# Half of the out projection between the halves of the gate projection, decayed B in front of the outputs, in a Mamba-style recurrent layer on Trainium2

## The chip, the cores and the metric

The kernel runs on one core of one Trainium2 chip. A core has a matrix engine (TensorE, PE in the profile), three engines that work on 128 partitions (VectorE or DVE, ScalarE or ACT, GpSimd or POOL) and a queue for transfers (SyncE or SP). Each runs its own instructions in program order, and they wait for one another on semaphores. The metric is the time of one execution on the device in microseconds; the smaller the better.

## What is computed

`u` has 4 sequences of 1024 tokens with 128 features. Each token is normalised and projected to a gate z and an input x of 2048 channels each (32 heads of 64), to B and C (64 each), and to angles, step sizes and mixing weights per head. Then, cut to what matters here:

```python
Bm, Cm = rope(_rms(Braw) + B_bias), rope(_rms(Craw) + C_bias)   # rotated by cumulative angles, per head
def step(carry, inp):
    h, prevBx = carry
    x_t, B_t, C_t, a_t, g_t, b_t = inp
    Bx = jnp.einsum('bhp,bhn->bhpn', x_t, B_t)
    h = a_t[..., None, None] * h + g_t[..., None, None] * Bx + b_t[..., None, None] * prevBx
    return (h, Bx), jnp.einsum('bhpn,bhn->bhp', h, C_t)
y = y + xh * D
y = y * silu(z)
y = _rms(y, norm_w)
s = y @ out_proj_w.T
out = u + s * silu(fp8_linear(xn))
```

## The kernel before

`prepare` does what is done once (normalisation, small projections, running sums of decays). `units` is the main loop and takes nearly all of the time. It cuts the 4096 tokens into NS = 8 tiles `t` of 512 tokens, each of four chunks of 128, and the 32 heads into NQ = 8 groups `q` of four heads, that is two pairs p = 0 and 1. There are 64 iterations (t, q). Two tiles make a sequence: an even tile begins one (its first chunk has no state to add), an odd tile ends one.

The recurrence is done by chunks. Per iteration the engines do this, each in the order written out by hand in its block:

- **VectorE**: `rotation` (L1299) makes the parts of rotated B and C: `part` from `bcs` and `trig`, both in SBUF, eight per iteration, for the next group. `angles` (L1274) reduces the angles of the group after that. `state` (L1373) carries the state over chunks, in six to eight small instructions. `x_scaled` (L1283) makes `xc` from x. `scores` (L1317) multiplies scores by decays to `M`, four per iteration (0, 1 are made one iteration ahead). L1412 makes `yT`, output times silu(z), one for each pair. `b_decayed` (L1309) makes `bw`, B times decay, two for the next group. `norm_start`, `norm_seeded` and `norm_refined` are small instructions for the norm of the tile before, in the iterations q = 0.
- **PE**: `angles` (L1107), the chunk states (L1193), `exponents` (L1127, one per head), `scores` (L1138, sixteen matmuls per pair), `x_by_token` (L1112, two halves), `project` (L1153, the out projection of the group before), z (L1221, two halves, one PSUM bank each, `R[0]` and `R[1]`, which x uses before them), the outputs y (L1229, L1235, L1245), and `b_by_token` (L1118), the transposes of rotated B. `square_sums` (L1164) adds the squares over partitions, once per tile.
- **ACT**: `decays` (L1458, to `E`), `x_copy` (L1463), silu of z (L1505), `sines` (L1447 to L1453), `rounding` (L1443), `squares` (L1468, of `yT`).
- **POOL**: `sums` (L1527) adds two parts to `rot`, four per iteration; `c_decayed` (L1536) makes `ce` from `rot` and `eb`, two; L1571 adds the squares to `sqa`, two (L1564 for q = 0, where it is one).
- **SP** issues the transfers: `spread` (trig, eight per iteration), `load_eb`, `load_rows` and others.

Around the change the order on VectorE is, for an iteration (t, q): rotation 0 of the next group, `angles`, `state`, rotation 1, xc 0, M 2, M 3, xc 1, rotations 2 to 7, yT 0, yT 1, bw 0, bw 1, M 0, M 1 of the next group. In the prediction, A is the first of these rotations and B the second. VectorE's semaphore waits for M are on `e_ready` (ACT's decay) and `s_ready` (PE's scores); for bw on `bt_ready`; for yT on `y_ready`, `sz_ready`, `out_ready`, `sq_ready`. z half p waits for `xk_ready`, that is for xc p, which reads the same bank.

## Time and profile before

| | us |
|---|---|
| median of 3 runs | 1199.95 (1198.5 to 1201.43) |
| the profiled execution | 1202.91 |
| its span, from first to last instruction | 1201.0 |
| PE busy | 1130.3 (94%) |
| DVE busy | 1131.8 (94%) |
| ACT busy | 818.6 (68%) |
| POOL busy | 755.2 (63%) |
| mean granted TensorE clock | 0.969 of full |

The main loop begins at about 145 us and ends at about 1195. A row of the timeline gives the start of an instruction in us from the span's start, how long it lasted (several of one kind that follow one another are one row, with their number behind the x), its engine, its line, what it writes and reads, and in brackets the idle time of the engine before it with what ended that. An instruction that had to wait for the shared SBUF access after it was issued shows this as a longer duration, and not as idle time. Engines issue an instruction some 0.04 to 0.08 us before the one ahead has ended, so two rows of an engine may overlap by that much.

### The profile page before, as it was taken

Reading aid. Unit: us, or ns where it says so; the run is one execution under the profiler, and the core shown is the slowest. Engines: PE = TensorE matmul, PEld = TensorE weight load, DVE = VectorE, ACT = ScalarE, POOL = GpSimd, SP = SyncE. Lnnn points to the kernel's source line nnn. Section 1 sums busy time; section 2 is a strip of 40 time slices with the busy share of each in tenths; the row PEclk is TensorE's granted clock in tenths of the full one; section 3 lists DMA queues with packets and bytes.
Section 4 is the critical chain, followed back from the end, with each engine's and each line's share of the span. In section 5 each row is a group of like instructions: output and inputs, shape, how many; then the busy total and the mean of one; then the engine's idle time right before and its main releaser. Section 6 shows DMA issues by size and latency. Waiting matters only on the chain.

```text
span 1201.0 us, 30402 instructions
## 1 busy us (share of the span) xinstructions
PE 1130.3 (94%) x11442; PEld 822.0 (68%) x11442; DVE 1131.8 (94%) x1796; ACT 818.6 (68%) x1270; POOL 755.2 (63%) x560
## 2 busy tenths in 40 slices
PE   3899599999999999999999999999999999999996
PEld 3673467777777777677777777777777777777675
DVE  7878599999999999999999999999999999999994
ACT  4678366767676676777666777667766766776663
POOL 5000256776776667666777677776766687767774
PEclk9956699999999999999999999999999999999999
DMA  8645645444545464545554464546544545444450
GB/s 184 213 137 123 146 108 115 117 113 110 139 100 115 106 152 106 125 97 124 125 124 106 101 148 101 123 111 145 115 108 103 136 115 125 107 93 99 111 120 15
DMA packets 91888, 142.94 MB, mean 119 GB/s; under 512 B 19326, under 2 KB 38591, under 8 KB 91327
## 3 DMA queue, kind: packets, MB, share of 16 engines
q1 hardware_dynamic: 91743, 141.00, 50.3%
q8 instruction: 91, 1.49, 0.5%
q14 instruction: 54, 0.44, 0.1%
HBM read 58.68 MB, written 13.37 MB: 60 GB/s over the span
## 4 chain that ended last, share of the span: by engine, by line
PE 56%; DVE 19%; issue 8%; DMA 2%; ACT 1%; SPq 1%; POOL 0%; DVEq 0%; POOLq 0%; ACTq 0%
PE y L1235 10%; PE r L1221 8%; PE s L1138 6%; PE y L1229 5%; PE r L1118 5%; PE o L1153 5%; PE y L1245 5%; PE r L1112 4%; DVE M L1317 4%; DVE hs L1373 4%; DVE xc L1283 3%; DVE bw L1309 3%; PE r L1193 2%; PE r L1107 2%; PE d L1127 2%
## 5 line engine op out<-in xcount | busy, mean ns | idle before, releaser
L1527 POOL TENSOR_TENSOR rot<-part 128x512 f32<-128x512 f32 x256 | 383.9, 1500 | 310.8 <-DVE part L1299 310.8
L1299 DVE SCALAR_TENSOR_TENSOR part<-k_bcs,k_prmT,k_trig 128x512 f32<-128x512 f32 x512 | 527.1, 1077 | 9.2 <-SPq L1047 6.3
L1458 ACT ACTIVATE E<-d 128x512 f32<-128x512 f32 x256 | 152.9, 597 | 184.4 <-PE d L1127 184.1
L1536 POOL TENSOR_TENSOR ce<-rot,eb 128x512 f32<-128x512 f32 x128 | 185.5, 1468 | 2.3 <-POOLq L1566 2.1
L1317 DVE TENSOR_TENSOR M<-s,E 128x512 f32<-128x512 f32 x256 | 163.6, 677 | 1.9 <-PE s L1138 1.4
L1571 POOL TENSOR_TENSOR sqa<-sqa,sq 128x512 f32<-128x512 f32 x112 | 142.7, 1274 | 31.7 <-ACT sq L1468 23.1
L1138 PE MATMUL s<-rot 64*128 64x128 f32 x2048 | 149.2, 285 | 0.0
L1138 PEld LDWEIGHTS s<-rot 64*128 64x128 f32 x2048 | 124.7, 188 | 35.2 <-issue 34.8
L1112 PE MATMUL r<-k_w_zx,k_xns 128*128 128x256 f32 x512 | 136.8, 391 | 11.8 <-issue 6.3
L1463 ACT COPY xk<-r 128x512 f32<-128x512 f32 x128 | 75.2, 587 | 104.7 <-PE r L1112 104.6
L1235 PE MATMUL y<-M,xk 128*64 128x128 f32 x2048 | 140.1, 279 | 0.0
L1153 PEld LDWEIGHTS o<-k_w_o,yT 128*128 128x128 f32 x1024 | 132.8, 192 | 8.5 <-DVE yT L1412 1.7
L1221 PE MATMUL r<-k_xns,k_w_zx 128*128 128x512 f32 x256 | 133.3, 614 | 4.0 <-DVE xc L1283 1.8
L1153 PE MATMUL o<-k_w_o,yT 128*128 128x128 f32 x1024 | 133.4, 275 | 1.4 <-DVE yT L1412 1.4
L1235 PEld LDWEIGHTS y<-M,xk 128*64 128x64 f32 x2048 | 109.2, 136 | 21.5 <-issue 21.5
L1112 PEld LDWEIGHTS r<-k_w_zx,k_xns 128*128 128x128 f32 x512 | 90.4, 192 | 30.3 <-DVE ang L1274 8.5
L1127 PE MATMUL d<-k_cum,k_pick 123*128 123x512 bf16 x256 | 99.4, 388 | 0.0
L1505 ACT ACTIVATE sz<-r 128x512 f32<-128x512 f32 x128 | 75.7, 597 | 33.0 <-PE r L1221 32.4
L1283 DVE TENSOR_TENSOR xc<-r,k_cc 128x512 f32<-128x512 f32 x128 | 87.2, 681 | 4.6 <-ACT xk L1463 4.6
L1193 PEld LDWEIGHTS r<-xk,bw 128*64 128x64 f32 x1792 | 57.5, 137 | 48.8 <-DVE bw L1309 47.3
L1229 PEld LDWEIGHTS y<-k_ident,xc 128*128 128x128 f32 x512 | 58.8, 140 | 44.7 <-issue 44.7
L1412 DVE TENSOR_TENSOR yT<-y,sz 128x512 f32<-128x512 f32 x128 | 81.7, 677 | 6.3 <-PE y L1245 6.3
(247 smaller groups left out, 1673.2 us busy)
## 6 DMA issues: line engine op xcount, KB each, us to landing
k_trig<-k_tri SPq DMA_DIRECT2D x512, 128.0 KB, 2.4
eb<-ecum_rows SPq DMA_DIRECT2D x128, 256.0 KB, 4.7
k_bcs<-bc_t SPq DMA_DIRECT2D x16, 256.0 KB, 3.9
k_bcs<-bc_t SPq DMA_DIRECT2D x32, 128.0 KB, 3.8
k_bcs<-in_L_attn_u SPq DMA_DIRECT2D x4, 512.0 KB, 6.4
xn_t<-a_xnT SPq DMA_DIRECT2D x1, 2048.0 KB, 12.7
tc_t<-a_tcT SPq DMA_DIRECT2D x1, 2048.0 KB, 17.2
bc_t<-a_tmp SPq DMA_DIRECT2D x1, 2048.0 KB, 7.5
```

The lines of the kernel that those rows point to most:

```text
L1112: last = nc.tensor.matmul(R[i][:, 256 * c:256 * c + 256], xns[:, (t + q // NQ) % 2, (2 * i + c) * P:(2 * i + c + 1) * P], K["w_zx"][:, DI ...
L1127: nc.tensor.matmul(Dp[:], K["pick"][:, head * P:head * P + P], K["cum"][0:D_ROWS, q % 2, h, :], start=True, stop=True).then_inc(d_ready, 1)
L1138: last = nc.tensor.matmul(Sp[j][:, k], rot[rows, q % 2, p, 0, k], rot[rows, q % 2, p, 1, k], start=True, stop=True)
L1153: last = nc.tensor.matmul(Op[:, k], yT[:, p, k], K["w_o"][:, (2 * q + p) * P:(2 * q + p + 1) * P], start=False, stop=q == NQ - 1 and c == ...
L1221: nc.tensor.matmul(R[p][:], w, xns[:, t % 2, :], start=True, stop=True).then_inc(z_ready, 1)
L1235: nc.tensor.matmul(Yp[p][m:m + 64, k], xk[:, par, c, 128 * p + m:128 * p + m + 64], M[:, 2 * p + j, k], start=False, stop=c == 0 and begin ...
L1299: nc.vector.scalar_tensor_tensor(out=part[:, 2 * p + f, :], in0=bcs[:, (t + q // NQ) % 2, 2 * w + f, :], scalar=col, in1=trig[:, p, 1 - f, ...
L1317: nc.vector.tensor_tensor(M[:, h, :], Sp[h % 2][:], E[:, h % 2, :], ALU.mult).then_inc(m_ready, 1)
L1458: nc.scalar.activation(E[:, h % 2, :], Dp[:], ACT.Exp).then_inc(e_ready, 1)
L1527: nc.gpsimd.tensor_tensor(rot[:, q % 2, p, w, :], part[:, 2 * p, :], part[:, 2 * p + 1, :], ALU.add).then_inc(rot_ready, 1)
L1536: nc.gpsimd.tensor_tensor(ce[:, p, :], rot[:, q % 2, p, 1, :], eb[:, p, :], ALU.mult).then_inc(ce_ready, 1)
L1571: nc.gpsimd.tensor_tensor(sqa[:], sqa[:], sq[:, p, :], ALU.add).then_inc(sqa_ready, 1)
```

## The change

No instruction is added or removed; five orders change.

- PE: `project(t, q - 1, (2, 3))`, half of the out projection (all of it for q = 1), stands between the two halves of z instead of ahead of both. `square_sums(t - 1)`, in the iterations q = 0, stands behind the first half of `project` instead of ahead of `x_by_token`.
- VectorE: `b_decayed` stands ahead of yT, and M 0, yT 0, M 1, yT 1 alternate. In q = 0 `norm_start` stands behind `x_scaled(…, 1)`, and the last `norm_refined` behind yT 0.
- ACT: `decays(q + 1, 1)` stands ahead of both squares. `rounding` is done for q + 3 between the two squares, where it was done for q + 2 at the start of the next iteration.
- POOL: `c_decayed` of the next group stands directly behind its sums and ahead of the additions of squares, where it stood behind them.

```diff
@@ tensor
-                    if q == 0 and t > 0:
-                        square_sums(t - 1)
                     if live(t, q + 1):
...
                         x_by_token(t, q + 1, 0)
                     if t + q > 0 and q != 1:
                         project(t, q - 1, (0, 1))
+                    if q == 0 and t > 0:
+                        square_sums(t - 1)
                     pe.wait_ge(hch, at(T8, t, 8 * q + 8))
                     if live(t, q + 1):
                         x_by_token(t, q + 1, 1)
-                    if t + q > 0:
-                        project(t, q - 1, (2, 3) if q != 1 else range(CS))
                     for p in range(2):
-
+                        if p == 1 and t + q > 0:
+                            project(t, q - 1, (2, 3) if q != 1 else range(CS))
                         if live(t, q + 1):
                             pe.wait_ge(xk_ready, at(T2, t, 2 * q + 2 + p + 1))
@@ vector
+                    if live(t, q + 1):
+                        x_scaled(t, q + 1, tn, 1)
                     if q == 0 and t > 0:
                         norm_start(t - 1)
-                    if live(t, q + 1):
-                        x_scaled(t, q + 1, tn, 1)
...
+                    if live(t, q + 1):
+                        b_decayed(t, q + 1, tn)
                     for p in range(2):
+                        if live(t, q + 1):
+                            scores(t, q + 1, p)
                         dve.wait_ge(sz_ready, at(T2, t, 2 * q + p + 1))
...
                         nc.vector.tensor_tensor(yT[:, p, :], Yp[p][:], sz[:, p, :], ALU.mult).then_inc(yt_ready, 1)
-                    if q == 0 and t > 0:
-                        norm_refined(t - 1, 2)
-                    if live(t, q + 1):
-                        b_decayed(t, q + 1, tn)
-                    if live(t, q + 1):
-                        scores(t, q + 1, 0)
-                        scores(t, q + 1, 1)
+                        if p == 0 and q == 0 and t > 0:
+                            norm_refined(t - 1, 2)
@@ scalar
+            rounding(0, 2)
             for t in range(NS):
                 for q in range(NQ):
-                    if live(t, q + 2):
-                        rounding(t, q + 2)
...
                     if live(t, q + 1):
                         decays(t, q + 1, 0)
+                        decays(t, q + 1, 1)
                     squares(t, q, 0)
-                    if live(t, q + 1):
-                        decays(t, q + 1, 1)
+                    if live(t, q + 3):
+                        rounding(t, q + 3)
                     squares(t, q, 1)
@@ gpsimd
+            c_decayed(0, 0)
             for t in range(NS):
                 for q in range(NQ):
-                    c_decayed(t, q)
                     if live(t, q + 1):
                         for k in range(4):
                             sums(t, q + 1, k)
...
+                        c_decayed(*((t, q + 1) if q < NQ - 1 else (t + 1, 0)))
                     if q == 0:
```

## Rows read from the trace of the kernel before

**Rows 1.** Windows: length, busy (count) of PE, PEld, DVE, ACT, POOL; clock, DMA share, GB/s.
```profile
614.06:630.36 16.30, 16.16 (x170) 11.62 (x170) 15.75 (x26) 11.15 (x18) 11.44 (x8) 1.00 0.51 129
745.06:761.23 16.17, 16.04 (x171) 11.64 (x170) 16.06 (x28) 11.30 (x18) 11.44 (x8) 1.00 0.56 133
```

**Rows 2.** Timeline of DVE in the iteration in an odd tile (start, duration, instruction).
```profile
613.98 6.09 DVE L1299 SCALAR_TENSOR_TENSOR part<-k_bcs,k_prmT,k_trig 128x512 f32<-128x512 f32 x6
620.00 1.28 DVE L1412 TENSOR_TENSOR yT<-y,sz 128x512 f32<-128x512 f32 x2
...
624.08 0.97 DVE L1299 SCALAR_TENSOR_TENSOR part<-k_bcs,k_prmT,k_trig 128x512 f32<-128x512 f32 x1 [0.41 <-DMA k_trig<-k_tri]
...
627.03 0.93 DVE L1299 SCALAR_TENSOR_TENSOR part<-k_bcs,k_prmT,k_trig 128x512 f32<-128x512 f32 x1
```

**Rows 3.** The same timeline, of POOL.
```profile
615.46 1.73 POOL L1527 TENSOR_TENSOR rot<-part 128x512 f32<-128x512 f32 x1 [2.44 <-DVE part L1299]
...
620.15 1.28 POOL L1527 TENSOR_TENSOR rot<-part 128x512 f32<-128x512 f32 x1 [0.63 <-DVE part L1299]
621.81 2.69 POOL L1571 TENSOR_TENSOR sqa<-sqa,sq 128x512 f32<-128x512 f32 x2 [0.38 <-ACT sq L1468]
624.47 2.95 POOL L1536 TENSOR_TENSOR ce<-rot,eb 128x512 f32<-128x512 f32 x2
```

**Rows 4.** The fourth of the six rotations of rows 2, alone.
```profile
615.96 1.77 DVE L1299 SCALAR_TENSOR_TENSOR part<-k_bcs,k_prmT,k_trig 128x512 f32<-128x512 f32 x1
```

**Rows 5.** Timeline of PE and ACT in the same iteration.
```profile
620.51 1.16 PE L1138 MATMUL s<-rot 64*128 64x128 f32 x16
622.03 0.60 ACT L1458 ACTIVATE E<-d 128x512 f32<-128x512 f32 x1 [0.30 <-PE d L1127]
622.53 0.62 ACT L1468 ACTIVATE sq<-yT 128x512 f32<-128x512 f32 x1
625.71 1.13 PE L1112 MATMUL r<-k_w_zx,k_xns 128*128 128x256 f32 x4
...
629.32 2.22 PE L1221 MATMUL r<-k_xns,k_w_zx 128*128 128x512 f32 x4
```

**Rows 6.** Timeline around 492 us, DVE and POOL.
```profile
492.30 1.84 DVE L1299 SCALAR_TENSOR_TENSOR part<-k_bcs,k_prmT,k_trig 128x512 f32<-128x512 f32 x1 [0.55 <-DMA k_trig<-k_tri]
492.33 2.94 POOL L1536 TENSOR_TENSOR ce<-rot,eb 128x512 f32<-128x512 f32 x2
```

**Rows 7.** Timeline of the start of the loop.
```profile
141.39 1.26 POOL L1527 TENSOR_TENSOR rot<-part 128x512 f32<-128x512 f32 x1 [0.63 <-DVE part L1299]
...
142.78 2.49 POOL L1536 TENSOR_TENSOR ce<-rot,eb 128x512 f32<-128x512 f32 x2
...
145.03 1.65 PE L1138 MATMUL s<-rot 64*128 64x128 f32 x16
...
146.76 0.69 DVE L1317 TENSOR_TENSOR M<-s,E 128x512 f32<-128x512 f32 x1 [1.36 <-PE s L1138]
```

**Rows 8.** Timeline of the iteration in an even tile.
```profile
751.30 1.16 PE L1138 MATMUL s<-rot 64*128 64x128 f32 x16
...
754.58 1.27 DVE L1299 SCALAR_TENSOR_TENSOR part<-k_bcs,k_prmT,k_trig 128x512 f32<-128x512 f32 x1
...
758.09 0.74 DVE L1299 SCALAR_TENSOR_TENSOR part<-k_bcs,k_prmT,k_trig 128x512 f32<-128x512 f32 x1
```

**Rows 9.** Timeline of a tile start, iterations q = 0 and 1.
```profile
267.84 0.68 DVE L1283 TENSOR_TENSOR xc<-r,k_cc 128x512 f32<-128x512 f32 x1
...
279.94 0.95 PE L1164 MATMUL y<-k_ones,sqa 128*128 128x1 f32 x8
...
284.39 0.68 DVE L1283 TENSOR_TENSOR xc<-r,k_cc 128x512 f32<-128x512 f32 x1
...
300.94 0.68 DVE L1283 TENSOR_TENSOR xc<-r,k_cc 128x512 f32<-128x512 f32 x1
301.51 1.88 PE L1221 MATMUL r<-k_xns,k_w_zx 128*128 128x512 f32 x4
```

## The prediction

> **What bounds the kernel now.** I read the totals first [rows 1]: within one iteration of the main loop TensorE is busy 16.16 of 16.30 us and VectorE 15.75. Two engines are full at once, so what matters is the loop of waits that joins them, and I read one iteration engine by engine. The profile calls the engines PE (TensorE), DVE (VectorE), ACT (ScalarE), POOL (GpSimd) and SP (SyncE). I count time inside an iteration from the end of its `x_scaled(…, 1)` (below: xc1): 614.06 in an odd tile, 745.06 in an even one. The two stretches of rows 1 run from there to the next xc1's end, so an iteration takes 16.30 and 16.17 us.
>
> The reader is to see three things in these rows.
>
> First, the eight `rotation` instructions don't cost one price. Undisturbed, one takes 0.74 [rows 8], and the six after xc1 would take 4.0 at that price; they took 6.09 [rows 2]. The fourth after xc1 took 1.77: it was issued at 615.96, while POOL's sum ran from 615.46 to 617.19 [rows 3, 4], and it ended 0.55 after that sum. A rotation reads two SBUF tiles, a POOL addition too, and in these rows one stands still until the other is through. POOL pays as well: 1.73 for that sum, 1.28 for the one at 620.15 with no rotation beside it. VectorE's other operations (yT, bw, M, xc, which read one PSUM tile) keep their 0.68 and follow one another every 0.60, also beside POOL: the two yT at 620.00 took 1.28 while POOL ran its sum of 620.15 [rows 2, 3]. So the order in which VectorE and POOL come to the shared access is a cost of its own.
>
> Second, the rotation that opens an iteration, A, is the one in question. It was issued at 624.08, while POOL added the squares (621.81 to 624.50), and ended at 625.05, again 0.55 behind POOL [rows 2, 3]. Although POOL's ce was next in its queue at 624.47, A went first, as it had been waiting: ce took 2.95 for two, not about 2.5.
>
> Third, what places the end of that addition: scores on PE end at 621.67, the last decay on ACT 622.03 to 622.63, the second square 622.53 to 623.15, then the addition, then A, and from A's end VectorE runs without a gap to xc1, which releases the second half of z [rows 2, 3, 5]. This is the loop: z, y, scores, decay, square, addition, A, xc1, 16.3 us.
>
> **What the change does to it, part by part.** PE: half of `project` goes between the halves of z. No instruction is added. The second half of z waits for xc1 as before, so PE only fills a wait of about 0.3 us there (the z group took 2.22 for four [rows 5], and 1.88 where nothing held it [rows 9]), and it is worth nothing while xc1 comes last. I take 0, bounds -0.3 and 0. The first silu on ACT comes earlier, and nothing waits for it.
>
> ACT: `rounding(q+3)` goes between the squares and `decays(q+1, 1)` ahead of both. Rounding needs PE's `angles(q+3)`, which needs only bw 0, now early; squares follow yT. The second square slips behind yT 1, and the decay that follows it by about 0.6 us; PE uses that decay only before its `x_by_token`, which waits longer for A. 0. SP: no DMA is added. `load_eb` waits for ce, which is now ready earlier in the iteration; SP comes to it after the eight spreading DMAs as before, and there is over half an iteration until the next ce. The k_trig transfer can hold A (0.41 us of idle at 624.08 [rows 2]) but A now comes at 10.1 against 10.02 there, so this falls away or lies under what holds A below: 0.
>
> VectorE: the order after the rotations was yT 0, yT 1, bw 0, bw 1, M 0, M 1, A. It becomes bw 0, bw 1, M 0, yT 0, M 1, yT 1, A. The same six operations, but M 0 now comes third and meets a wait that the trace of before does not show: it needs the scores. VectorE would be ready at 5.94 + 1.20 = 7.14 [rows 2]. The sixteen score matmuls end at 621.67 - 614.06 = 7.61 in an odd tile and 752.46 - 745.06 = 7.40 in an even one [rows 5, 8]. From the end of such a group to M it was 146.76 - 146.68 = 0.08 at the start of the loop, the one place where M waited for scores [rows 7]. So M 0 starts at 7.69 (odd), 7.48 (even), a wait of 0.55 and 0.34. Then yT 0, M 1, yT 1 and A follow at 0.60 each: **A is issued at 10.09 and 9.88**. In before it was ready to go at about 9.5 (9.52 even [rows 8]). The queue behind M 0 is the whole of VectorE. Bounds for this wait alone: 0 (if the scores are seen before 7.14) and 0.6.
>
> POOL: ce moves from behind the squares' additions to directly behind the sums. The last sum ends at 620.15 + 1.28 - 614.06 = 7.37 [rows 3]; the even tile has the same, as its rotations end at the same place (A issued at 9.52, six operations of 0.60 before it: 5.92 [rows 8], against 5.94). How ce follows a sum directly is shown at the start: sum ends 142.65, ce starts 142.78, two take 2.49 [rows 7]. So **ce ends at 9.99**, and the first addition of squares can be issued at about 9.95 (POOL issues 0.03 to 0.04 ahead of an end: 624.47 against 624.50 [rows 3]). It is ready by then: yT 0 ends at 7.69 + 0.60 + 0.68 = 8.97, its square takes 0.62 [rows 5] and the hand-overs about 0.12, so 9.7.
>
> So the new orders bring A (10.09 and 9.88) and the first addition of squares (9.95) to the shared access at the same moment. In the odd tile the addition is first by 0.14. In the even tile A is issued 0.07 before it. Which wins there is told by one event in the trace: at 492.30 a late rotation was issued 0.03 ahead of POOL's ce at 492.33, and lost. It took 1.84, to 494.14, which is 0.55 after ce's first half [rows 6]. A blocked rotation ends 0.55 after its release, an undisturbed one 0.74 after its issue, so it seems to ask only some 0.19 after its issue: 10.07 in the even tile, too late against 9.99. I take it that A loses in both.
>
> The Trainium skill (SBUF — State Buffer, "Who interferes with whom") calls this an exclusive lock between VectorE operations with two SBUF inputs and GpSimd, where "Issue order, not op shape, decides who blocks." The blocked rotations agree with the lock; the pair at 492.30 does not agree with a literal issue order. By that sentence A would pass in even tiles, which is the first rival below.
>
> If A loses, the addition runs 9.95 to 11.22 and A ends at 11.77, in both kinds of tile. Before: 10.99 odd, 10.79 even. From A's end to B, the second rotation, 1.98 odd and 2.24 even; B now undisturbed at 0.74 (odd: was 0.93, held by ce, so 0.19 comes back); from B's end to xc1's end 2.40 [rows 1, 2, 8].
> - odd: 11.77 + 1.98 + 0.74 + 2.40 = 16.89, against 16.30: **+0.59**
> - even: 11.77 + 2.24 + 0.74 + 2.40 = 17.15, against 16.17: **+0.98**
>
> PE is not the limit: it now waits about 0.9 for A's follower before `x_by_token`.
>
> Tile starts: `square_sums` (0.95 of PE [rows 9]) now stands after half of `project`. With A late, PE goes from 12.4 (behind VectorE's `angles`, 0.68, that follows A) through x, out, x, out (625.71 to 629.32, 3.6 [rows 5]), the sums (0.95) and half of z (0.9) to z 1 at 17.8. Before, this iteration took 16.55 from xc1 to xc1 (268.52 to 285.07 [rows 9]): +1.2. In the next one (301.62 - 285.07 = 16.55 too) z already ended 1.77 behind xc1 (303.39) instead of 1.2, so 17.1 from z to z. There all of `project` now stands between the z halves, and z 0 waits for xc 0, which waits for ACT's copy behind `normalised`: an estimate of 17.6, +0.5. POOL has only one addition in that iteration, which waits for the second square, so A passes. The iteration after makes good 0.2. Together +1.5 per start; bounds 0.5 and 2.5.
>
> **Sum.** Even tiles have 4 x 6 such iterations (q = 2 to 7), odd tiles 3 x 6, and the last 5: 24 x 0.98 = 23.5 and 23 x 0.59 = 13.6; seven starts x 1.5 = 10.5; the accident at 492.30 (that iteration was 1.2 longer) goes: -1.2. Total +46.4. The profiled execution took 1202.9, 3.0 over the median of 1199.95; so 1249.3 profiled and **1246 us** for the median.
>
> **Rivals.**
> - *A passes in even tiles.* A ends at 9.99 + 0.55 = 10.54, xc1 at 10.54 + 2.24 + 0.74 + 2.40 = 15.92: -0.25 an iteration, about what PE still allows: it was idle only 0.14 of 16.30 by its records [rows 1], beside the wait in the z group. 24 x -0.25 in place of 23.5 gives 1217. As PE then comes after xc1 by up to 0.1, the next A is issued at 9.98 and loses; if they alternate, 1231. For it: the margin is 0.07 to 0.19 us. Against it: 492.30. Chance 0.14.
> - *A passes everywhere.* Odd: A 10.09 to 10.83, B is held by the second addition; about -0.15; even -0.25; starts +1.3 each for PE's reason: 1200, no change. Needs POOL 0.14 to 0.3 later than the startup row says. Chance 0.05.
> - *Faster: M 0 does not wait.* If the scores are ready for M 0 at 7.14, A is issued at 9.54, is already waiting when ce ends at 9.99, and passes ahead of the addition as at 624.50. It ends at 10.54, and both kinds of iteration fall to what PE allows, about 16.0: 23 x -0.3 + 24 x -0.17 = -11, and starts at +0.8: +5.6. 1194 to 1195. It decides at an A issued before about 9.8, that is scores 0.1 (even) to 0.3 (odd) us earlier than their rows. Against it: those rows are the same in all iterations but tile starts. With other ways to be faster that I don't see, chance 0.15.
> - *Slower still*: tile starts at their upper bound, or the second addition takes B too: 1254 to 1262. Chance 0.06.
>
> **How the numbers follow.** Forecast 0.60, rivals as given. About 0.2% (2.4 us) is what a measurement of this kernel tells from no change. Slower: 0.60 + 0.14 + 0.06 = 0.80; same 0.05; faster 0.15. The likeliest case alone spans 1236 to 1256 (starts, and 0.1 us on each iteration). The range for 8 in 10 reaches down through the even-tile rival: 1210 to 1256.
>
> **What would show it.** In the profile after: M 0 with an idle time of 0.3 to 0.6 released by PE's scores; A lasting 1.6 to 1.9 instead of 0.97 to 1.27, beside the first addition of squares; ce 2.5 for two, directly behind the last sum; B at 0.74; iterations of 16.9 (odd) and 17.15 (even) with PE idle 0.8 to 0.9 before `x_by_token`. It is wrong if A shows under 1.3 in most iterations, or if M 0 has no idle time.

## The result, and the profile after

| | before | after |
|---|---|---|
| median (runs) | 1200.69 (1196.88 to 1205.29, 6) | 1228.52 (1225.74 to 1234.78, 6) |
| ratio, with its 95% interval | | 1.0242 (1.0214 to 1.027) |
| span of the profiled execution | 1201.0 | 1232.6 |

The change makes the kernel 2.4% slower. That is inside the range of 1210 to 1256, but 17.5 us below the forecast of 1246 and outside the 1236 to 1256 that the prediction gave to its likeliest case. The first lines of the page of after, then four groups of its section 5:

```profile
span 1232.6 us, 30401 instructions
PE 1124.6 (91%) x11442; PEld 824.1 (67%) x11442; DVE 1132.8 (92%) x1796; ACT 819.5 (66%) x1270; POOL 749.7 (61%) x560
...
L1298 DVE SCALAR_TENSOR_TENSOR part<-k_bcs,k_prmT,k_trig 128x512 f32<-128x512 f32 x512 | 518.1, 1058 | 6.5 <-SPq L1047 6.3
...
L1316 DVE TENSOR_TENSOR M<-s,E 128x512 f32<-128x512 f32 x256 | 169.5, 682 | 23.4 <-issue 21.4
L1570 POOL TENSOR_TENSOR sqa<-sqa,sq 128x512 f32<-128x512 f32 x112 | 162.1, 1448 | 22.3 <-ACT sq L1466 14.3
L1534 POOL TENSOR_TENSOR ce<-rot,eb 128x512 f32<-128x512 f32 x128 | 160.7, 1277 | 8.5
```

Busy times hardly differ from those of before; what has grown is idle time. The line to look at is M: 23.4 us of idle time in front of it, nearly all put down to issue. Before, it was 1.9:

```profile
L1317 DVE TENSOR_TENSOR M<-s,E 128x512 f32<-128x512 f32 x256 | 163.6, 677 | 1.9 <-PE s L1138 1.4
```

In after no instruction is named as the releaser, but the timelines below put M's start 0.09 behind the end of the scores: it is the wait that the prediction spoke of. ce takes 1.28 each: POOL's ce is no longer beside a rotation.

The whole spans are not good to compare. The loop begins (end of the first xc1) at 137.7 us in before and at 141.6 in after; over the profiles of this case it begins anywhere from 131.4 to 141.6, and the TensorE clock granted in the first 131 us goes with it (0.77 in before, 0.76 in after, 0.82 in e6, which begins at 131.4). So from here on I sum the loop alone, from the end of the first xc1 to that of the last: 1032.46 before, 1059.50 after, **+27.0**, which agrees with the +27.8 between the medians. Iteration by iteration (63 of them, from one xc1 end to the next; groups of four heads by q):

| part of the loop | before, each | after, each | predicted, sum | measured, sum |
|---|---|---|---|---|
| odd tiles, q = 3 to 7 (19) | 16.30 | 16.91 (mean) | +11.2 | +11.5 |
| even tiles, q = 3 to 7 (20) | 16.17 and one of 17.39 | 16.12 | +18.4 | -2.1 |
| q = 0, 1 and 2 (24) | 16.59 (mean) | 17.33 (mean) | +16.8 | +17.6 |
| all | | | +46.4 | +27.0 |

(The predicted sums are those of the prediction, distributed: 19 x 0.59; 20 x 0.98 less the accident's 1.2; the starts' 10.5 with 4 x 0.98 + 4 x 0.59 for q = 2.) The odd tiles came out as worked out, the even tiles did not lose at all, and the third line is near only as a sum, as the section on the prediction shows.

Windows of one iteration in an odd and one in an even tile of after, columns as in [rows 1]:

```profile
628.23:645.13 16.90, 15.93 (x172) 11.67 (x171) 16.32 (x27) 11.20 (x18) 11.24 (x8) 1.00 0.51 126
763.40:779.51 16.11, 15.82 (x172) 11.69 (x171) 15.71 (x27) 11.18 (x17) 11.52 (x8) 1.00 0.55 128
```

The odd one, timeline of VectorE and POOL, with PE's scores and x (xc1 ends at 628.23), answering to [rows 2, 3, 5]:

```profile
634.32 1.27 POOL L1525 TENSOR_TENSOR rot<-part 128x512 f32<-128x512 f32 x1 [0.63 <-DVE part L1298]
...
634.69 1.16 PE L1138 MATMUL s<-rot 64*128 64x128 f32 x16
...
635.72 2.51 POOL L1534 TENSOR_TENSOR ce<-rot,eb 128x512 f32<-128x512 f32 x2
...
635.94 0.69 DVE L1316 TENSOR_TENSOR M<-s,E 128x512 f32<-128x512 f32 x1 [0.44 <-issue]
...
638.20 2.94 POOL L1570 TENSOR_TENSOR sqa<-sqa,sq 128x512 f32<-128x512 f32 x2
638.34 1.67 DVE L1298 SCALAR_TENSOR_TENSOR part<-k_bcs,k_prmT,k_trig 128x512 f32<-128x512 f32 x1
...
640.66 1.13 PE L1112 MATMUL r<-k_w_zx,k_xns 128*128 128x256 f32 x4 [0.64 <-DVE ang L1273]
...
641.99 0.74 DVE L1298 SCALAR_TENSOR_TENSOR part<-k_bcs,k_prmT,k_trig 128x512 f32<-128x512 f32 x1
```

The even one (xc1 ends at 763.40), answering to [rows 8]:

```profile
769.64 1.16 PE L1138 MATMUL s<-rot 64*128 64x128 f32 x16
...
770.88 2.51 POOL L1534 TENSOR_TENSOR ce<-rot,eb 128x512 f32<-128x512 f32 x2
770.89 0.69 DVE L1316 TENSOR_TENSOR M<-s,E 128x512 f32<-128x512 f32 x1 [0.29 <-issue]
...
773.29 0.74 DVE L1298 SCALAR_TENSOR_TENSOR part<-k_bcs,k_prmT,k_trig 128x512 f32<-128x512 f32 x1
...
773.34 3.23 POOL L1570 TENSOR_TENSOR sqa<-sqa,sq 128x512 f32<-128x512 f32 x2
...
776.27 0.85 DVE L1298 SCALAR_TENSOR_TENSOR part<-k_bcs,k_prmT,k_trig 128x512 f32<-128x512 f32 x1
```

Read the two side by side. In the odd tile the addition of squares is issued at 638.20 and A at 638.34. A is second: it takes 1.67 and ends, at 640.01, 0.54 after the first addition (638.20 + 1.27). PE waits 0.64 behind VectorE's `angles`, and the iteration is 16.9. In the even tile A is issued at 773.29, 0.05 ahead of the addition's 773.34. A takes 0.74, and it is the addition that pays (3.23 for two). In the even tile B also pays a little (0.85), held by the second addition.

### The profile page after: what moved, and what is told of

Read it like the earlier page. It is cut to its first block, busy times and chain, and to the rows that moved or that the text cites. A ratio compares the mean times of both kernels' runs of the same rounds, so it can differ in the third digit from the quotient of the medians.

```text
span 1232.6 us, 30401 instructions
## 1 busy us (share of the span) xinstructions
PE 1124.6 (91%) x11442; PEld 824.1 (67%) x11442; DVE 1132.8 (92%) x1796; ACT 819.5 (66%) x1270; POOL 749.7 (61%) x560
## 4 chain that ended last, share of the span: by engine, by line
PE 54%; DVE 16%; issue 14%; ACT 2%; DVEq 1%; DMA 0%; POOL 0%; SPq 0%; POOLq 0%; ACTq 0%
PE y L1234 10%; PE r L1220 10%; PE o L1153 7%; PE y L1228 5%; PE r L1118 5%; PE y L1244 5%; PE r L1112 5%; DVE yT L1415 4%; PE s L1138 4%; DVE ang L1273 3%; DVE hs L1372 2%; DVE xc L1282 2%; DVE M L1316 2%; PE d L1127 1%; DVE part L1298 1%
## 5 line engine op out<-in xcount | busy, mean ns | idle before, releaser
L1298 DVE SCALAR_TENSOR_TENSOR part<-k_bcs,k_prmT,k_trig 128x512 f32<-128x512 f32 x512 | 518.1, 1058 | 6.5 <-SPq L1047 6.3
L1316 DVE TENSOR_TENSOR M<-s,E 128x512 f32<-128x512 f32 x256 | 169.5, 682 | 23.4 <-issue 21.4
L1570 POOL TENSOR_TENSOR sqa<-sqa,sq 128x512 f32<-128x512 f32 x112 | 162.1, 1448 | 22.3 <-ACT sq L1466 14.3
L1534 POOL TENSOR_TENSOR ce<-rot,eb 128x512 f32<-128x512 f32 x128 | 160.7, 1277 | 8.5
L1220 PE MATMUL r<-k_xns,k_w_zx 128*128 128x512 f32 x256 | 138.6, 623 | 8.5 <-DVE xc L1282 7.4
L1127 PE MATMUL d<-k_cum,k_pick 123*128 123x512 bf16 x256 | 99.5, 389 | 15.8 <-ACT E L1456 13.2
L1466 ACT ACTIVATE sq<-yT 128x512 f32<-128x512 f32 x128 | 80.7, 631 | 39.2 <-DVE yT L1415 38.9
L1415 DVE TENSOR_TENSOR yT<-y,sz 128x512 f32<-128x512 f32 x128 | 86.9, 679 | 6.3 <-PE y L1244 6.3
L1308 DVE TENSOR_TENSOR bw<-r,k_dec 128x512 f32<-128x512 f32 x128 | 82.0, 679 | 10.2 <-PE r L1118 10.1
```

The costliest lines, as they stand in the source:

```text
L1220: nc.tensor.matmul(R[p][:], w, xns[:, t % 2, :], start=True, stop=True).then_inc(z_ready, 1)
L1298: nc.vector.scalar_tensor_tensor(out=part[:, 2 * p + f, :], in0=bcs[:, (t + q // NQ) % 2, 2 * w + f, :], scalar=col, in1=trig[:, p, 1 - f, ...
L1316: nc.vector.tensor_tensor(M[:, h, :], Sp[h % 2][:], E[:, h % 2, :], ALU.mult).then_inc(m_ready, 1)
L1415: nc.vector.tensor_tensor(yT[:, p, :], Yp[p][:], sz[:, p, :], ALU.mult).then_inc(yt_ready, 1)
L1534: nc.gpsimd.tensor_tensor(ce[:, p, :], rot[:, q % 2, p, 1, :], eb[:, p, :], ALU.mult).then_inc(ce_ready, 1)
L1570: nc.gpsimd.tensor_tensor(sqa[:], sqa[:], sq[:, p, :], ALU.add).then_inc(sqa_ready, 1)
```

## The experiments

Ratios are against the kernel before, in the same job, with 95% intervals; loop sums are from the profile of each kernel. "Lost" and "passed" are said of A at the shared access.

**e1: M behind yT.** The change with one order undone: VectorE does yT 0, M 0, yT 1, M 1, so that nothing waits for scores ahead of yT.

```diff
                     for p in range(2):
-                        if live(t, q + 1):
-                            scores(t, q + 1, p)
...
                         nc.vector.tensor_tensor(yT[:, p, :], Yp[p][:], sz[:, p, :], ALU.mult).then_inc(yt_ready, 1)
...
+                        if live(t, q + 1):
+                            scores(t, q + 1, p)
```

> The changed kernel, with yT 0, M 0, yT 1, M 1 on VectorE in place of M 0, yT 0, M 1, yT 1. Theory (the loss in odd tiles is the wait of M 0 for the scores, which makes A miss the shared access): M 0 is due at 7.74 and finds its scores; A is issued at 9.54, waits for ce to end at 9.99 and passes ahead of the addition, ends at 10.54. B is then held by the second addition to 13.5, so iterations of odd and even tiles both go to 15.9 to 16.1 (now 16.91 and 16.12). About 17 to 20 us less than the changed kernel, about 1210. Rival (half of project between the halves of z costs the time, by making z and so y later): odd iterations stay at 16.9, 1228.

Measured: 1205.4 (1203.48 to 1212.33, 5 runs), ratio 1.0071 (1.0041 to 1.0101). The loop sum is 1036.80: 22.7 of the 27.0 are gone with this one order, where 17 to 20 were expected. By the ratios of the whole times it is 1.7% of the 2.4%, about 20 us. Odd and even iterations from q = 3 on are 16.03 to 16.20, but for two of 16.91 (odd) and one of 17.17 (even). Such a single one and its neighbour, timeline of VectorE and POOL:

```profile
623.81 2.94 POOL L1570 TENSOR_TENSOR sqa<-sqa,sq 128x512 f32<-128x512 f32 x2
623.83 1.79 DVE L1298 SCALAR_TENSOR_TENSOR part<-k_bcs,k_prmT,k_trig 128x512 f32<-128x512 f32 x1 [0.33 <-DMA k_trig<-k_tri]
...
638.53 0.68 DVE L1316 TENSOR_TENSOR M<-s,E 128x512 f32<-128x512 f32 x1
...
640.33 0.98 DVE L1298 SCALAR_TENSOR_TENSOR part<-k_bcs,k_prmT,k_trig 128x512 f32<-128x512 f32 x1
...
640.72 3.14 POOL L1570 TENSOR_TENSOR sqa<-sqa,sq 128x512 f32<-128x512 f32 x2
```

The M at 638.53 has no idle time in front. A at 640.33 comes 0.39 ahead of the addition; it waits for ce to end and passes. At 623.83 a transfer of trig kept A for 0.33, it came 0.02 behind the addition, and took 1.79. So a delay of A by 0.33 makes an iteration 0.86 longer: this is the mechanism of the forecast, once with the wait and once without.

**e2: the addition waits for both squares.** The change as it is, but POOL's first addition of squares comes later, so that A is first in every tile.

```diff
-                        pool.wait_ge(sq_ready, at(T2, t, 2 * q + p + 1))
+                        pool.wait_ge(sq_ready, at(T2, t, 2 * q + 2))
```

> The changed kernel, with the first addition of squares on POOL waiting for both squares instead of one. Nothing is faster by itself, and M 0 still waits for the scores. Theory (A loses the shared access to an addition issued 0.14 us ahead of it): the addition now comes at 10.9, A (10.11) passes and ends at 10.85 in odd tiles too; the second addition then holds B to about 14.0, so odd iterations 16.4 (now 16.91), even ones 16.1 to 16.2 (now 16.12): 8 to 10 us less, about 1219. Rival (the wait of M 0 alone makes the loss, whoever passes first): odd iterations stay at 16.9 or grow.

Measured: 1223.23 (1222.83 to 1226.76, 4 runs), ratio 1.0214 (1.0188 to 1.024); loop sum 1053.34, 6.2 less than the change, where 8 to 10 were expected. Odd iterations 16.56 (16.91 in the change; 16.4 expected), even 16.34 (16.12). Timeline of an odd one:

```profile
618.25 0.74 DVE L1298 SCALAR_TENSOR_TENSOR part<-k_bcs,k_prmT,k_trig 128x512 f32<-128x512 f32 x1
...
619.07 2.68 POOL L1570 TENSOR_TENSOR sqa<-sqa,sq 128x512 f32<-128x512 f32 x2 [0.85 <-ACT sq L1466]
...
620.97 1.33 DVE L1298 SCALAR_TENSOR_TENSOR part<-k_bcs,k_prmT,k_trig 128x512 f32<-128x512 f32 x1
```

A passes (0.74) in the iterations from q = 3 on, which is the cause tested. But the two additions now run 619.07 to 621.75 and B, at 620.97, stands 0.59 for the second. The cost of the shared access has moved to the next instruction of VectorE that needs it. The loop is still 20.9 longer than before although A never loses: 6.5 of it from q = 3 on, 14.4 in q = 0 to 2.

**e3: POOL's order alone.** The kernel before, with ce directly behind the sums.

```diff
                 sums(0, 0, k)
+            c_decayed(0, 0)
             for t in range(NS):
                 for q in range(NQ):
-                    c_decayed(t, q)
...
+                        c_decayed(*((t, q + 1) if q < NQ - 1 else (t + 1, 0)))
                     if q == 0:
```

> The kernel before, with ce behind the sums and ahead of the additions on POOL, and nothing else. Theory: A is issued at 9.52, waits for ce to 9.99, ends at 10.54 in place of 10.99 and 10.79; the two additions then run to 13.0 and hold B to 13.5. Iterations 15.9 to 16.1 in both kinds of tile, 0.1 to 0.3 less than before: 8 to 15 us less than before, about 1188. Rival (ce early is itself a part of the loss): slower than before, by up to the 17 us that odd tiles lost.

Measured: 1213.34 (1213.15 to 1224.1, 4 runs), ratio 1.0147 (1.01 to 1.0193). From q = 3 on iterations take 16.03 to 16.15 but for three of 16.90 to 17.00, as expected; the total is not. The loop is 14.2 longer than before, and more than all of that is in q = 0, where from the second tile on iterations take 18.45 to 20.0. Timeline of one, POOL and PE:

```profile
274.05 3.12 POOL L1572 TENSOR_TENSOR sqa<-sqa,sq 128x512 f32<-128x512 f32 x2
...
277.31 1.02 PE L1164 MATMUL y<-k_ones,sqa 128*128 128x1 f32 x8 [1.66 <-POOL sqa L1572]
```

The additions end at 277.17 and PE, which needs them for `square_sums` ahead of `x_by_token`, has stood idle for 1.66. This edge was missing from my expectation. It is what the change moves `square_sums` for.

**e9: POOL's order with the sums of squares later.** e3, with `square_sums` behind the first half of `project` and `norm_start` behind xc1, as in the change; VectorE's orders around M, yT and bw, ACT's and z's stay those of before.

```diff
-                    if q == 0 and t > 0:
-                        square_sums(t - 1)
...
                         project(t, q - 1, (0, 1))
+                    if q == 0 and t > 0:
+                        square_sums(t - 1)
```

> The kernel before, with ce ahead of the additions on POOL, square_sums behind the first half of project and norm_start behind x_scaled; VectorE's order of yT, bw and M, ACT's order and project as before. Theory: the iterations q = 3 to 7 stay at 16.05 (with ce alone they were 16.05, before 16.16 and 16.30), and q = 0, which took 18.5 to 20.0 with ce alone as PE waited there for the additions, goes to 16.6 to 16.9. 6 to 10 us less than before, 1190. Rival (q = 0 loses for another reason): it stays above 18.

Measured: 1195.39 (1190.21 to 1202.93, 12 runs), ratio 0.9977 (0.995 to 1.0004); loop sum 1024.20, 8.3 less than before. q = 0 takes 16.6 to 16.7 from the second tile on, and q = 2 to 7 take 16.02 to 16.14 but for one of 17.17. By the one profile this part of the change gains 0.22 an iteration in odd tiles and 0.09 in even ones besides the accident; in the whole time that is at the edge of what can be told, as the interval reaches 1. Executions with the same granted clock agree on the sign: at 0.975, three of e9 took 1190.21 to 1192.68 and seven of before 1196.48 to 1199.36.

**e4, e8, e11: A put off by a small operation.** The change, with a memset on VectorE ahead of A, of 32, 160 and 320 columns, that nothing else uses. This is to find where between "0.05 ahead" and "0.14 behind" A begins to lose.

```diff
+        pad = sb("pad", [P, 160])
...
                             norm_refined(t - 1, 2)
+                    nc.vector.memset(pad[:], 0.0)
```

> The changed kernel, with one memset of a small unused tile (32 columns) on VectorE ahead of A in each iteration, about 0.1 us. Theory (in even tiles A passes only because it is issued 0.07 ahead of the addition): A comes at 10.0, loses, and even iterations jump from 16.12 to 17.1 to 17.2, twenty-odd times; odd ones by 0.1 at most. 20 us more than the changed kernel, about 1250. Rival (even tiles pass for another reason, for instance because they have no carried state to add): both kinds grow by the 0.1 us of the memset, 5 to 6 us in all, about 1234.

> The changed kernel with a memset of 160 columns ahead of A on VectorE, which should take about 0.2 and put A off by about 0.15, where the one of 32 columns put it off by only some 0.04. Theory: A is now issued behind the addition in even tiles too, and loses: even iterations go from 16.13 to 17.1 to 17.3, odd ones from 16.91 by at most 0.15. 20 us more than the changed kernel. Rival: both kinds grow by 0.15.

> The changed kernel with a memset of 320 columns ahead of A (about 0.33 us by the 0.19 of 160 columns and 0.085 of 32). With 160 columns A still passed in even tiles except in the first tile, where it was 0.1 us behind the addition and those iterations took 17.17 against 16.17. Theory: A is now behind by 0.15 or more everywhere, loses everywhere, and the even iterations q = 3 to 7 of all tiles take 17.2 to 17.4; odd ones stay near 16.9 to 17.1, as they lost already. Rival (the first tile differs for another reason): the even iterations of the later tiles grow by the 0.13 of the memset alone, to 16.3.

Measured: e4 1230.16 (1227.6 to 1239.49, 4 runs), ratio 1.0289 (1.0238 to 1.0341): the memset put A off by only about 0.04, A stayed 0.03 to 0.05 ahead of the addition in most even iterations (0.10 to 0.13 in the others that passed), and those stayed at 16.13 to 16.19; two of the twenty lost (17.17 and 17.25). That is a miss by itself. e8: 1241.72 (2 runs), ratio 1.0351 (1.0298 to 1.0403). e11, 1 run: 1235.21. The loop sums are 1063.15, 1065.67 and 1069.77, that is 3.6, 6.2 and 10.3 over the change. Timeline of two even iterations of e8:

```profile
219.69 0.19 DVE L1419 MEMSET pad<- 128x160 f32 x1
219.70 2.96 POOL L1572 TENSOR_TENSOR sqa<-sqa,sq 128x512 f32<-128x512 f32 x2
219.80 1.72 DVE L1299 SCALAR_TENSOR_TENSOR part<-k_bcs,k_prmT,k_trig 128x512 f32<-128x512 f32 x1
...
747.46 0.19 DVE L1419 MEMSET pad<- 128x160 f32 x1
747.53 3.20 POOL L1572 TENSOR_TENSOR sqa<-sqa,sq 128x512 f32<-128x512 f32 x2
747.57 0.63 DVE L1299 SCALAR_TENSOR_TENSOR part<-k_bcs,k_prmT,k_trig 128x512 f32<-128x512 f32 x1
```

At 219.80 A is 0.10 behind and loses, as in the even iterations of tile 0 (17.17). At 747.57 it is 0.04 behind and passes, as in those of tiles 2, 4 and 6 (16.17). In e11 17 of the 20 even iterations were 16.34, with A 0.18 or more behind; I had expected 17.2 to 17.4 there. Over all iterations of a kernel, by the recorded starts, A needs to be 0.03 ahead in e4, may be 0.10 behind in e8 and 0.27 behind in e11. In e8 the start of the memset tells it better. Of the iterations where it lies within 0.25 of POOL's, A passed in 18 of 18 where the memset began 9 ns or more ahead, and lost in all 28 where it began less than 5 ns ahead (as at 219.69, which the rows round to 0.01) or behind; in e11 the boundary is at a memset some 0.03 behind, with two exceptions. So behind a memset A's own start does not say when the access was claimed.

The memset alone does not hold the access for A. Where A's last transfer of trig was late, A lost although the memset was well ahead. The even iteration of 17.25 in e4, timeline of VectorE and POOL:

```profile
1003.78 0.09 DVE L1419 MEMSET pad<- 128x32 f32 x1
...
1003.90 1.83 DVE L1299 SCALAR_TENSOR_TENSOR part<-k_bcs,k_prmT,k_trig 128x512 f32<-128x512 f32 x1
1003.91 1.27 POOL L1572 TENSOR_TENSOR sqa<-sqa,sq 128x512 f32<-128x512 f32 x1
```

The memset began 0.13 ahead of the addition, but the last packet of trig landed only at 1003.87, and A lost. The two exceptions of e11 are of the same kind: at 736.29 the memset began 0.06 ahead of the addition, as in five iterations that passed, but in these trig had landed 0.28 or more before the memset, and here it landed with the memset's start. By these rows A's claim needs A's own data, and it can be made while the memset still runs; A's duration fits that (0.74 alone, 0.72 behind 32 columns, 0.63 behind 160 and 320). What sets the moment of the claim there is **open**.

**e5: the out projection back.** The change, with all of `project` ahead of both halves of z again.

```diff
+                    if t + q > 0:
+                        project(t, q - 1, (2, 3) if q != 1 else range(CS))
                     for p in range(2):
-                        if p == 1 and t + q > 0:
-                            project(t, q - 1, (2, 3) if q != 1 else range(CS))
```

> The changed kernel, with all of the second part of project ahead of both halves of z again, as before the change. Theory (the project between the halves costs nothing in most iterations, but in q = 1, where all 16 matmuls stand there, it makes z 1 late and with it the next iteration): odd iterations q = 3 to 7 stay at 16.85 to 16.91 and even ones at 16.1; q = 1 goes from 17.69 (odd) to about 17.0 and q = 2 from 17.75 to 16.9 (odd) and 17.79 to 16.2 (even). 8 to 12 us less than the changed kernel. Rival (project between the halves is what costs the odd iterations): they fall to 16.3, and 20 us or more are gained.

Measured: 1225.86 (1220.84 to 1229.21, 4 runs), ratio 1.0215 (1.0175 to 1.0254); loop sum 3.9 less than the change. Odd iterations stay 16.91 and even ones, but for one of 17.18, 16.12: the place of `project` has no part in them. q = 2 gives 5.2 (odd tiles 17.75, now 16.91 to 17.26; even ones 17.8 to 18.1, now 17.2 to 17.6, where A still loses), and the one of 17.18 takes 1.1 of it. A saving of 8 to 12 was expected.

**e6: e1, and for q = 1 the out projection ahead of z.**

```diff
+                    if q == 1:
+                        project(t, q - 1, range(CS))
                     for p in range(2):
-                        if p == 1 and t + q > 0:
-                            project(t, q - 1, (2, 3) if q != 1 else range(CS))
+                        if p == 1 and t + q > 0 and q != 1:
+                            project(t, q - 1, (2, 3))
```

> The variant with yT ahead of M, and besides for q = 1 alone all of project ahead of both halves of z. Theory: q = 1 goes from 16.98 to about 16.6 and q = 2 from 17.2 to 16.1, seven and eight times, all else as it was: 9 to 11 us less than without this, 1195, level with the kernel before or 0.3% faster. Rival (the tile starts lose for the later square_sums): q = 1 and 2 stay, and q = 0 is where the time is.

Measured: 1197.54 (1191.67 to 1203.97, 12 runs), ratio 0.9989 (0.9966 to 1.0012); loop sum 1027.48, 9.3 less than e1 and 5.0 less than before. q = 2 went from 17.2 to 16.1, but for two (16.91, 17.16). q = 1 stayed at 16.98 to 17.01, where 16.6 was expected.

**e10: the last norm instruction behind M 1.** e6, with `norm_refined(t - 1, 2)` behind both M. This asks what holds q = 1.

```diff
-                        if p == 0 and q == 0 and t > 0:
-                            norm_refined(t - 1, 2)
                         if live(t, q + 1):
                             scores(t, q + 1, p)
+                    if q == 0 and t > 0:
+                        norm_refined(t - 1, 2)
```

> The variant with yT ahead of M and project of q = 1 ahead of z, with the last norm_refined (128x4) behind M 1 in place of behind yT 0. Theory (this small instruction reads two SBUF tiles, and ce on POOL holds it for about 1 us at a tile start): it costs under 0.3 there, and the iterations q = 1 go from 16.98 to 16.6 or less, seven times; the others stay. Rival (the 17.0 of q = 1 is due to PE's project and ACT's normalised): they stay at 17.0.

Measured, 1 run: 1204.47; odd tiles' q = 1 fell from 16.98 to 16.13 in three of four. But other iterations grew (17.39 in even tiles' q = 1; 16.91 to 17.2 in q = 2, and one of 18.47), and the loop sum is 1034.01, 6.5 over e6. In the odd tiles the term is shown; without it the queue meets other collisions elsewhere.

**e12 and e13: the second addition of squares in the next iteration.** e9, with POOL's second addition behind the first sum of the next iteration; e13 also has half of `project` between the halves of z, but for q = 1.

```diff
                             sums(t, q + 1, k)
+                            if k == 0 and q > 1:
+                                added(t, q - 1, 1)
...
-                    for p in range(2):
...
+                    for p in range(2 if q == NQ - 1 else 1):
+                        added(t, q, p)
```

> The kernel before with ce ahead of the additions, square_sums and norm_start later, and besides the second addition of squares on POOL behind the first sum of the next iteration (for q = 1 to 6). Theory: in the variant without this, B is held by the second addition, which ends at 13.0; with it gone B ends at 13.3 in place of 13.5 to 13.7, and iterations go from 16.05 to between 15.85 and 16.0, where PE alone sets them. 3 to 8 us less than that variant, 1187 to 1192, ratio 0.990 to 0.995. Rival (PE sets the 16.05 already): no change.

> The one before, with half of project between the halves of z, except for q = 1. Theory: with VectorE no longer late, PE's wait for xc 1 between the z halves (up to 0.3 us) is what the split fills: 0 to 0.15 per iteration less than without it, so 0 to 8 us. Rival (the split is worth nothing, as z 1 still waits for xc 1, or costs): same or slower.

Measured: e12 1199.91 (12 runs), ratio 0.9991 (0.9971 to 1.0011); e13 1200.85 (12 runs), ratio 1.0002 (0.9983 to 1.0021). e12 misses the expectation of 0.990 to 0.995: its loop sum is 1031.51, 7.3 more than e9. e13, expected 0 to 8 below e12, has 1033.47. In odd tiles q = 5 to 7 take 15.77 (16.05 in e9), with the split and without it but for two that grew, so the split of `project`, the first item of the change, is worth nothing here either. In tiles after the first, q = 3 and 4 grow to 16.77 and 17.03. Timeline of POOL around one in tile 1, and the second of VectorE's six rotations there:

```profile
328.73 1.27 POOL L1527 TENSOR_TENSOR rot<-part 128x512 f32<-128x512 f32 x1 [1.67 <-DVE part L1299]
...
329.96 1.27 POOL L1554 TENSOR_TENSOR sqa<-sqa,sq 128x512 f32<-128x512 f32 x1
...
331.19 1.72 POOL L1548 TENSOR_TENSOR res<-so,res 128x512 f32<-128x512 f32 x1
...
331.70 1.76 DVE L1299 SCALAR_TENSOR_TENSOR part<-k_bcs,k_prmT,k_trig 128x512 f32<-128x512 f32 x1
```

There the last operations of the tile before (`so` and `res`) come behind the same sum, and the addition pushes them back. In e9 `res` starts at 328.51, beside xc and M, and VectorE's second rotation takes 0.74; here it starts at 331.19, and that rotation stands until 0.55 behind its end. That is the 1.0 by which these iterations are longer than q = 5 to 7. In tile 0 there are none, and its q = 3 and 4 take 16.03.

## Why the prediction came out as it did

**M 0 waits for the scores: right.** Predicted at 7.69 (odd) and 7.48 (even) from xc1's end; measured 635.94 - 628.23 = 7.71 and 770.89 - 763.40 = 7.49. e1 shows that this wait is what costs: without it 22.7 of the loop's 27.0 us go. The 0.08 from the start of the loop [rows 7] was a good price for a wait that the loop did not show.

**Odd tiles: right, for the reason given.** Predicted: A issued at 10.09, addition at 9.95, A's end at 11.77, iteration 16.89. Measured: 10.11, 9.97, 11.78, 16.90. The rule "0.55 behind the release" held, and B was undisturbed at 0.74.

**Even tiles: wrong. The failed step is the one that read a single event.** The positions were right (A at 9.88, measured 773.29 - 763.40 = 9.89; addition at 9.94). From the rotation at 492.30, issued 0.03 ahead of ce and beaten [rows 6], I inferred that a rotation asks for the access only some 0.19 after its issue, and so gave A the loss at a lead of 0.07. In the twenty even iterations from q = 3 on A led by 0.05 to 0.17 (14 of them by 0.05 to 0.08) and passed. The 0.19 was the difference of two durations (0.74 and 0.55), and no row showed it as a time of asking; the event itself said only that a lead of 0.03 is too little. The eleven traces without a memset have 164 rotations that start within 0.2 us of a POOL operation other than the sums:

| start of the rotation | passed | lost |
|---|---|---|
| behind, or up to 0.04 ahead | 0 | 85 |
| 0.05 or 0.06 ahead | 6 | 1 |
| 0.07 to 0.2 ahead | 72 | 0 |

Nine of the 85 were 0.02 to 0.04 ahead, as at 492.30. The one exception and one that passed at the same lead, timelines of e1 and of e6:

```profile
408.54 1.87 DVE L1298 SCALAR_TENSOR_TENSOR part<-k_bcs,k_prmT,k_trig 128x512 f32<-128x512 f32 x1 [0.25 <-DMA k_trig<-k_tri]
```

```profile
664.30 0.75 DVE L1300 SCALAR_TENSOR_TENSOR part<-k_bcs,k_prmT,k_trig 128x512 f32<-128x512 f32 x1 [0.25 <-DMA k_trig<-k_tri]
```

(POOL's addition starts at 408.60 and at 664.36.) A further 1408 rotations led one of POOL's sums by 0.07 to 0.17, with POOL idle ahead of it, and all passed. So, but for behind a memset, the order of the starts decides, with VectorE needing a lead of about 0.05 by the record. For a rotation that had not waited for trig (A in most iterations; the one at 492.30 had) the bound is wider: one lost at a lead of 0.02, the next passed at 0.05, and none lies between. The true case was one of hundredths, and the rival "A passes in even tiles", at 0.14, is what happened; that the range reached down to it kept the result inside, not the likeliest case. The Trainium skill (SBUF — State Buffer, "Who interferes with whom") says that issue order decides who blocks; the traces agree with that to 0.05 us, and the event at 492.30 lies inside this tolerance. It was no ground to put the rule second. A likeliest case built on the rule would have been 1217 to 1231.

**The size of that rival: too favourable.** I priced it at -0.25 an iteration; measured -0.05. A ends at 10.63 instead of 10.54: it took its undisturbed 0.74 from its issue at 9.89, where the working had it end 0.55 behind ce. And B was held: the additions begin when A is done and the second one runs until about 13.2, so B takes 0.85 and not 0.74. The working had kept the second addition for the odd tiles only.

**Tile starts: the sum near by luck, two causes of it not seen.** Predicted 16.8 for q = 0 to 2, measured 17.6. By parts it is not near: q = 0 and 1 lost 7.1 where seven times 1.2 and 0.5 were predicted (11.9), and q = 2 lost 10.5 where 4.9 was (6.3 for A, less seven times 0.2). Timeline of q = 1 in tile 1, VectorE, POOL and PE, answering to [rows 9]:

```profile
297.37 2.51 POOL L1534 TENSOR_TENSOR ce<-rot,eb 128x512 f32<-128x512 f32 x2
...
298.65 1.25 DVE L1341 SCALAR_TENSOR_TENSOR nrm<-tch,nrm 128x4 f32<-128x4 f32 x1
...
300.56 1.16 PE L1138 MATMUL s<-rot 64*128 64x128 f32 x16 [0.85 <-DVE M L1316]
...
306.67 0.68 DVE L1282 TENSOR_TENSOR xc<-r,k_cc 128x512 f32<-128x512 f32 x1
306.79 1.95 PE L1153 MATMUL o<-k_w_o,yT 128*128 128x128 f32 x16
...
308.57 1.02 PE L1220 MATMUL r<-k_xns,k_w_zx 128*128 128x512 f32 x2
```

The same small instruction in before:

```profile
292.42 0.18 DVE L1342 SCALAR_TENSOR_TENSOR nrm<-tch,nrm 128x4 f32<-128x4 f32 x1
```

An instruction of four columns stands 1.25 instead of 0.18. It reads two SBUF tiles, was issued 0.05 behind the start of ce's second half and ends 0.02 behind its end; and it holds M 1, for which PE then waits 0.85. So it is in the four odd tiles (1.23 to 1.25). In the three even ones it took 0.21 to 0.24: at 436.16 it was issued while ce's first half ran, and went between the two halves. I had placed it at no cost; e10 shows its price, 0.85 in three odd tiles. And all of the out projection for q = 1 between the halves of z puts the second half 1.22 behind xc1's end (308.57 - 307.35), which e6 takes back in the next iteration (17.2 to 16.1). In even tiles q = 1 was shorter than before (16.44 against 16.78). The sum came out near the forecast by errors of both signs.

**PE's split of the out projection at nothing: right.** e5 and e13 find no iteration from q = 3 on that it changes. **POOL's order: a gain that I had not priced alone.** By itself, with `square_sums` and `norm_start` moved, it is worth 8.3 us of the loop in e9's profile, though the ratio's interval there reaches 1; in the change the wait in M 0 spends it, and more.

## What to carry to other kernels

When two engines share an access that one of them holds alone, work out the issue times of both to a few hundredths of a microsecond and compare them; that order decides, and on which side of about 0.05 the margin lies is worth 0.9 to 1.0 us an iteration here (16.05 against 16.91 in e1, 16.13 against 17.17 in e4). An operation moved out of one collision can meet the next (B in e2, the second rotation in e12), so the whole iteration has to be worked out again. An instruction that has to wait, put early in the queue of an engine that is full, moves everything behind it, and its cost may be twice its own wait (0.44 of idle time, and 0.86 more an iteration than in e1, through a collision four operations later). One event gives a bound, not a size: 492.30 said "more than 0.03", and I made 0.19 of it; and compare loops iteration by iteration, as what lies ahead of it differed by up to 10 us between runs.

## What the runs showed of the hardware beyond expectation

- The shared access stops tiny operations too: 128x4 with two SBUF inputs took 1.25 when issued 0.05 behind the start of one of POOL's ce, 0.18 without, and 0.22 when it could go between two of them.
- A VectorE operation that already waits goes ahead of POOL's next queued one even where POOL's operations follow without a gap: A at 640.33 in e1 was issued while ce ran and went ahead of the addition at 640.72. POOL does not keep the access between its instructions.
- The tie is not at equal starts: a rotation lost at leads of 0.02 to 0.04 nine times in nine, and won at 0.07 to 0.2 72 times in 72, and 1408 times in 1408 against the sums.
- Behind a memset, a rotation whose recorded start was 0.04 to 0.27 behind POOL's still went first (e8, e11), but not where its trig landed as late as the memset's start (e4 at 1003.90, e11 at 736.29). The memset alone does not hold the access for it; what sets the moment of its claim is open.
